# Attention and expert layers on one core: the value products of a head set in one visit instead of three

## The chip, the cores and the metric
One core of one Trainium2 chip runs the whole program. The metric is the device time of one execution in microseconds (us); the median of the runs is given. TensorE, VectorE, ScalarE, GpSimd and SyncE each run their own in-order stream and meet through semaphores.

## The reference, cut to what matters
Input x is 4 batches of 512 tokens with 128 channels, fp32. Attention has 16 heads of 8 channels, causal, with a slope per head added to the key position:

```
x = x + attention(layernorm(x)) ; x = x + ffn(layernorm(x))
scores = q k^T / sqrt(8) + slope[h] * key_position, masked above the diagonal
attn = softmax(scores);  y = attn v;  y @ w_proj + b_proj
ffn: top-1 gate of 8 experts is used only as a factor near 1;
     sum over all experts of gelu(z @ w1[e] + b1[e]) @ w2[e] + b2[e], times that factor
```

## The kernel before, in words
**Steps.** The kernel walks over batches b (4) and over sets s of four heads (4 sets, called SETS; the four heads of a set are its QUADS). One (b, s) is a step, n = 4b + s, so there are steps 0 to 15. Each step has 16 places; a plan written out by hand says at which place TensorE issues what. For set n the step does:

- twelve exponential units (`exp_unit`, lines 754 and 760): scores transposed (keys on partitions) into a bank of `a_ring` (three PSUM banks), a mask matmul in bf16 on top (line 760), and then ScalarE's exponential into `probs` (line 559). Four units (one for each head) make a kind. Kind 0 is key block 0 (512 query columns), kind 1 key blocks 1 and 3 (384 + 128), kind 2 key block 2 (256).
- the value products (`pv`, line 779): `probs` times `v_ones` (values and a column of ones for the denominator), 128 x 32 weights, four heads side by side in four column tiles of TensorE, into the one bank `pv_bank`. Two consecutive sets share the bank. fp32 matmuls are issued as two instructions each, so kind 0 is 8, kind 1 is 16 and kind 2 is 8 instructions.
- twelve maximum units for the set after it (`max_unit`, line 732): scores with queries on partitions into a bank of `v_ring` (three PSUM banks), and VectorE's maximum along the keys (line 1066, a custom instruction and a read-out of its accumulator for each query block). When all twelve are done, `transpose_max` (line 741, 16 columns of weights) turns the maxima, VectorE makes `m_hi` and `m_lo` (lines 1083, 1084), and SyncE's queue writes them into `q_stack` (line 389) for the next step's exponential units.
- parts of other batches (`side`): projection of the next batch's q, k, v (lines 685 to 687, with transposes on line 696), the transposes and the projection of y (lines 792, 799, 808), z (layer norm output, transposed on line 816, split by VectorE into `zT_hi` and `zT_lo` on lines 962 and 963), logits, and the FFN of the batch before: `ffn1` (three matmuls for each 128-column tile, lines 685 to 687, into `a_ring`, GELU on ScalarE, line 576) and `ffn2` (line 847, fp32). In steps 5 and later, `ffn1` tiles 0 and 1 of a step are at place 1, tiles 2 and 3 at place 2, tile 4 at place 4. Steps with b >= 1 and s = 2 have one tile; steps 13, 14, 15 have 2, 2 and 4. Tile 0 of a batch is in s = 1, and z is transposed at place 15 of s = 0 (steps 4, 8, 12).

Within a place the order on TensorE is: side work, maximum units, `transpose_max`, exponential units, `pv`. Steps 0 to 4 follow `EARLY_PLAN`, the others `LATER_PLAN`. In `LATER_PLAN` the last maximum unit is at place 11, the ninth exponential unit at 12, `transpose_max` at 13, the last exponential unit at 15.

**Value products now.** Kind 0 is issued at place 12 (11 in the early plan), kind 1 at place 15, and kind 2 (`pv_last`) at place 0 of the next step. A visit waits until the exponentials of its kind are done (`e_freed`). After the last kind `pv_done` is raised; ScalarE copies the bank after every second set (`evacuate_pv`, line 566), and the exponentials of set n wait for the `pv_done` of set n - 2, since `probs` has two buffers.

After step 15 come the remaining FFN tiles of batch 2, the y work of batch 3, and the whole FFN of batch 3.

Of the kernel before, what the change touches and what calls it, by code (L numbers as in the profile page):

```python
# [35 lines left out]
P = 128  # L36
QUADS = 4
QR = P // QUADS
# [8 lines left out]
KINDS = 3  # L47
# [15 lines left out]
PLACES = 16  # L63
EARLY_PLAN = {
    "max": (-1, 0, 2, 3, 4, 5, 6, 8, 8, 9, 11, 11), "take_max": (12,),
    "exp": (4, 4, 5, 6, 8, 8, 9, 11, 11, 13, 14, 14), "pv": (11, 15), "pv_last": (0,),
}
LATER_PLAN = {
    "max": (-1, -1, 2, 3, 4, 5, 6, 7, 8, 9, 10, 11), "take_max": (13,),
    "exp": (4, 5, 6, 7, 8, 9, 10, 10, 12, 13, 14, 15), "pv": (12, 15), "pv_last": (0,),  # L70
}

STAGES = {
# [25 lines left out]
def block_kernel(nc, x, w_attn, w_proj, w1, w2, columns, rows, consts, out):  # L99
    B, T, C = x.shape  # L100
# [4 lines left out]
    TB = T // P  # L105
    SETS = H // QUADS
    UNITS = KINDS * QUADS
# [8 lines left out]
    KEY_BLOCKS = [[0], [1, 3], [2]]  # L116
    KIND_AT = [0, 512, 1024]
    PCOLS = 1280

    with ExitStack() as ctx:  # L120
        def sb(name, shape, dt=F32):
            return ctx.enter_context(nc.sbuf_tensor(name, shape, dt))

        def bank(name):
            return ctx.enter_context(nc.psum_tensor(name, [P, 512], F32))

        def sem(name):
            return ctx.enter_context(nc.semaphore(name))
# [50 lines left out]
        v_ones = [sb(f"v_ones{i}", [P, TB, SETS, QUADS, QR]) for i in range(2)]  # L179
# [6 lines left out]
        probs = sb("probs", [P, 2, QUADS, PCOLS])  # L186
# [32 lines left out]
        pv_bank = bank("pv_bank")  # L219
# [29 lines left out]
        e_freed = sem("e_freed")  # L249
# [13 lines left out]
        pv_done = sem("pv_done")  # L263
# [27 lines left out]
        def next_set(b, s):  # L291

            return (b, s + 1) if s < SETS - 1 else (b + 1, 0)

        def plan(n):
            return EARLY_PLAN if n <= SETS else LATER_PLAN

        def planned(b, s, k, what):

            return [unit for unit, place in enumerate(plan(SETS * b + s)[what]) if place == k]  # L300

        def maxima_due(n, k):


            units = []
            for ahead in (1, 2):
                for unit, place in enumerate(plan(n + ahead - 1)["max"]):
                    at = place if (n + ahead) % SETS else max(place, 0)
                    if at == k - PLACES * (ahead - 1) and n + ahead < SETS * B:
                        units.append(((n + ahead) // SETS, (n + ahead) % SETS, unit))  # L310
            return units
# [350 lines left out]
        def _(pe):  # L662
# [55 lines left out]
            def max_unit(b, s, k):  # L718
                if k == 0 and b < 2 and s == 0:
                    pe.wait_ge(q_const, SETS * (b + 1))  # L720
                if k == 0 and b == 0 and s % 2 == 0:
                    pe.wait_ge(k_const, QUADS * (s // 2 + 1))
                if k == 0:
                    pe.wait_ge(q_loaded, q_count(b + 1))
                q, kind = k // KINDS, k % KINDS
                if kind == 0 and s % 2 == 0:
                    pe.wait_ge(k_loaded[s // 2][q], K_LOADS * (b + 1))
                    pe.wait_ge(k_low_loaded[s // 2][q], K_LOW_LOADS * (b + 1))
                dst = v_bank()
                at = 0  # L730
                for n in MAX_BLOCKS[kind]:
                    last = pe.matmul(dst[:, at:at + P * (n + 1)], q_stack[b % 2][:, s, n * P:(n + 1) * P],  # L732
                                     k_stack[:, s, q, 0:P * (n + 1)], start=True, stop=True)
                    at += P * (n + 1)
                last.then_inc(v_filled, 1)

            def transpose_max(b, s):
                n = SETS * b + s
                pe.wait_ge(max_ready, n + 1)
                dst = v_bank()  # L740
                pe.transpose(dst[0:TB * QUADS, 0:P], row_max[:, n % 2, :], ident).then_inc(v_filled, 1)  # L741
# [19 lines left out]
                          start=False, stop=True, skip_group_check=True).then_inc(e_filled, 1)  # L761


            def pv(b, s, kind):
                n = SETS * b + s
                pe.wait_ge(e_freed, UNITS * n + QUADS * (kind + 1))
                if kind == 0 and s == 0:
                    pe.wait_ge(v_ready, b + 1)
                    if b == 0:
                        pe.wait_ge(v_const, 2)  # L770
                    if b == 1:
                        pe.wait_ge(v_const, 4)
                if kind == 0 and s % 2 == 0 and n >= 2:
                    pe.wait_ge(pv_evacuated, n // 2)
                at = KIND_AT[kind]
                for j in KEY_BLOCKS[kind]:
                    cols = P * (TB - j)
                    for q in range(QUADS):
                        last = pe.matmul(pv_bank[QR * q:QR * (q + 1), j * P:T], v_ones[b % 2][:, j, s, q, :],  # L779
                                         probs[:, n % 2, q, at:at + cols],  # L780
                                         start=(s % 2 == 0 and j == 0), stop=(s % 2 == 1 and j == 2),
                                         tile_position=(0, QR * q), skip_group_check=True)
                    at += cols
                if kind == KINDS - 1:
                    last.then_inc(pv_done, 1)


            def transpose_y(b, half):
# [68 lines left out]
            def side(b, s, k):  # L857

                for stage, of in due(STAGES, b, s, k, B):
                    if stage == "y_low":  # L860
                        transpose_y(of, 0)
                    if stage == "y_high":
                        transpose_y(of, 1)
                    if stage == "y_norm":
                        transpose_y_norm(of)
                    if stage == "attention":
                        project_y(of)
                    if stage == "z":
                        transpose_z(of)
                    if stage == "logits":  # L870
                        logits(of)
                    if stage == "ffn":
                        transpose_ffn(of)
                    if stage == "x":
                        transpose_x(of)
                    if stage == "q":
                        project_qk(of, 0)
                    if stage == "k":
                        project_qk(of, 1)
                    if stage == "v":  # L880
                        project_v(of)
                fb, tiles = chunk(b, s)
                for m, at in zip(tiles, FFN1_AT):
                    if k == at:
                        ffn1(fb, m)
                for m, at in zip(tiles, FFN2_AT):
                    if k == at:
                        ffn2(fb, m)
# [12 lines left out]
            for b in range(B):  # L901
                for s in range(SETS):
                    n = SETS * b + s
                    for k in range(PLACES):
                        side(b, s, k)
                        for unit in maxima_due(SETS * b + s, k):
                            max_unit(*unit)
                        if planned(b, s, k, "take_max") and next_set(b, s)[0] < B:
                            transpose_max(*next_set(b, s))
                        for unit in planned(b, s, k, "exp"):  # L910
                            exp_unit(b, s, unit)
                        for kind in planned(b, s, k, "pv"):
                            pv(b, s, kind)
                        if planned(b, s, k, "pv_last") and n >= 1:
                            pv((n - 1) // SETS, (n - 1) % SETS, KINDS - 1)
            pv(B - 1, SETS - 1, KINDS - 1)

            tiles = range(sum(LAST_TILES), NT)
            for i, m in enumerate(tiles):
# [380 lines left out]
```

## Time and profile before

| | |
|---|---|
| median of 3 runs | 323.85 us (323.07 to 324.44) |
| the profiled execution's own time | 324.16 us |
| its span, first to last instruction | 322.4 us |
| TensorE (PE) busy in the span | 291.8 us, 91% |
| VectorE (DVE), ScalarE (ACT) busy | 190.1 us (59%), 193.9 us (60%) |
| `pv` matmuls (line 779) | x512, 42.3 us, mean 440 ns |
| granted TensorE clock, mean | 0.998 |

The span is 1.8 us shorter than the execution's time. Busy time of matmuls overlaps and has modelled ends, so the distance between the starts of two neighbouring rows is the better measure of what an instruction costs. Steps 0 to 15 run from about 36 us to 273 us of the span.

### The profile page before, as it was taken

What the parts mean: (1) busy time and instruction counts of PE and PEld (TensorE: products, weight loads), DVE (VectorE), ACT (ScalarE), POOL (GpSimd) and SP (SyncE); (2) the same over time, 40 slices, a digit from 0 to 9 for tenths busy, and PEclk for the clock granted to TensorE, in tenths of its full rate; (3) what the DMA queues carried; (4) which work ended last, traced back from release to release, by engine and by line L of the source; (5) the groups of instructions that cost most, each with busy time, mean ns of one, the idle gap of its engine ahead of it and who ended that gap; (6) DMA issues with size and microseconds to landing.
All of it is one profiled execution on the core that took longest, in us unless ns stands there. A gap on an engine that the chain in (4) does not pass through costs nothing.

```text
span 322.4 us, 5513 instructions
## 1 busy us (share of the span) xinstructions
PE 291.8 (91%) x1784; PEld 191.4 (59%) x1784; DVE 190.1 (59%) x788; ACT 193.9 (60%) x323; POOL 76.1 (24%) x211
## 2 busy tenths in 40 slices
PE   0638799999969999999999999999999999999993
PEld 0435465666646666667666676657667655655651
DVE  4528479778777768564777785647776711451011
ACT  6462245556447468758577397767587786525362
POOL 3349312520133055002321181020300500000120
PEclk9999999999999999999999999999999999999999
DMA  6254300130300013003000140011001000000001
GB/s 181 91 146 121 134 4 0 33 123 2 92 29 0 0 39 123 3 0 100 19 3 2 35 142 19 2 34 49 3 3 37 0 4 0 0 2 4 30 0 33
DMA packets 12524, 13.23 MB, mean 41 GB/s; under 512 B 2064, under 2 KB 9104, under 8 KB 12240
## 3 DMA queue, kind: packets, MB, share of 16 engines
q1 hardware_dynamic: 11376, 11.70, 12.0%
q0 software_dynamic: 1024, 1.05, 1.6%
q8 instruction: 14, 0.23, 0.3%
q10 hardware_dynamic: 96, 0.13, 0.2%
q14 instruction: 14, 0.11, 0.1%
HBM read 5.14 MB, written 1.05 MB: 19 GB/s over the span
## 4 chain that ended last, share of the span: by engine, by line
PE 81%; DVE 10%; DMA 3%; issue 2%; ACT 1%; SPq 1%; DVEq 0%; ACTq 0%
PE ffn_bank L847 17%; PE a_ring L754 12%; PE v_ring L732 12%; PE pv_bank L779 11%; PE a_ring L685 5%; PE a_ring L760 5%; PE a_ring L687 4%; PE a_ring L686 4%; DVE unused L1066 4%; PE v_ring L808 1%; DMA q_stack<-q_lo 1%; PE v_ring L685 1%; PE v_ring L741 1%; DMA q_stack<-m_lo 1%; PE v_ring L686 1%
## 5 line engine op out<-in xcount | busy, mean ns | idle before, releaser
L1066 DVE CUSTOM_DVE_ANT_0 unused<-v_ring,cst 128x512 bf16<-128x512 f32 (+3 forms) x256 | 112.1, 487 | 52.1 <-PE v_ring L732 48.0
L559 ACT ACTIVATE probs<-a_ring 128x512 f32<-128x512 f32 (+1 forms) x192 | 92.4, 526 | 67.6 <-PE a_ring L760 66.6
L732 PE MATMUL v_ring<-k_stack,q_stack 128*128 128x512 f32 (+3 forms) x256 | 88.5, 417 | 7.3 <-DMA q_stack<-q_lo 5.1
L754 PE MATMUL a_ring<-q_stack,k_stack 128*128 128x512 f32 (+3 forms) x256 | 76.6, 359 | 2.0 <-DMA q_stack<-m_lo 2.0
L847 PE MATMUL ffn_bank<-hidden,w_sb 128*128 128x512 f32 x128 | 66.3, 602 | 1.1 <-ACT ffn_T L585 0.8
L732 PEld LDWEIGHTS v_ring<-k_stack,q_stack 128*128 128x128 f32 x256 | 48.6, 206 | 27.5 <-issue 17.1
L576 ACT ACTIVATE hidden<-a_ring,cols_sb 128x512 f32<-128x512 f32 x64 | 43.4, 688 | 32.5 <-PE a_ring L687 32.0
L754 PEld LDWEIGHTS a_ring<-q_stack,k_stack 128*128 128x128 f32 x256 | 46.5, 196 | 9.5 <-issue 5.6
L760 PE MATMUL a_ring<-score_mask,ident_bf 128*128 128x128 bf16 (+1 forms) x192 | 47.9, 251 | 0.0
L779 PE MATMUL pv_bank<-probs,v_ones 128*32 128x256 f32 (+3 forms) x512 | 42.3, 440 | 0.0
L685 PE MATMUL a_ring<-zT_hi,w_hi 128*128 128x512 f32 x64 | 33.0, 516 | 0.8 <-DVEq L965 0.8
L326 POOL DMA_DIRECT2D k_stack<-k_lo x32 | 18.1, 568 | 56.3 <-PE a_ring L760 51.6
L760 PEld LDWEIGHTS a_ring<-score_mask,ident_bf 128*128 128x128 bf16 x192 | 18.7, 97 | 20.5 <-issue 13.1
L687 PE MATMUL a_ring<-zT_hi,w_lo 128*128 128x512 f32 x64 | 25.2, 393 | 0.0
L686 PE MATMUL a_ring<-zT_lo,w_hi 128*128 128x512 f32 x64 | 25.1, 393 | 0.0
L847 PEld LDWEIGHTS ffn_bank<-hidden,w_sb 128*128 128x128 f32 x128 | 21.5, 192 | 5.9 <-ACT hidden L576 3.1
L1066 DVE DVE_READ_ACCUMULATOR2_ANT row_max<- 128x1 f32 x256 | 21.3, 83 | 0.0
L685 PEld LDWEIGHTS a_ring<-zT_hi,w_hi 128*128 128x128 f32 x64 | 12.1, 188 | 11.3 <-issue 7.1
L779 PEld LDWEIGHTS pv_bank<-probs,v_ones 128*32 128x32 f32 x512 | 12.3, 109 | 9.8 <-issue 6.5
L332 POOL TENSOR_SCALAR var<-mean_square 128x4 f32<-128x4 f32 x4 | 0.8, 188 | 69.5 <-DVE mean_square L1132 69.4
L576 ACT ACT_TABLE_LOAD x13 | 16.7, 1283 | 0.2
L686 PEld LDWEIGHTS a_ring<-zT_lo,w_hi 128*128 128x128 f32 x64 | 12.1, 189 | 4.8 <-issue 3.6
(110 smaller groups left out, 289.5 us busy)
## 6 DMA issues: line engine op xcount, KB each, us to landing
q_stack<-q_hi SPq DMA_DIRECT2D x8, 256.0 KB
k_stack<-k_hi SPq DMA_DIRECT2D x60, 32.0 KB
x_in<-x SPq DMA_DIRECT2D x4, 256.0 KB, 4.0
hidden<-w SPq DMA_DIRECT2D x1, 1024.0 KB, 8.3
k_stack<-k_lo POOLq DMA_DIRECT2D x32, 32.0 KB, 2.3
q_stack<-q_lo SPq DMA_DIRECT2D x4, 256.0 KB
w_sb<-w SPq DMA_DIRECT2D x1, 1024.0 KB, 5.1
x_res<-x SPq DMA_DIRECT2D x4, 256.0 KB, 3.6
```

Source lines behind the costliest of these rows:

```text
L326: queue.dma_start(k_stack[ROW_Q * q + g::ROW_D, 2 * half:2 * half + 2, q, :].bitcast(F32), part[rows:rows + QR // 2, :].bitcast(F32)).then ...
L559: act.activation(probs[:, n % 2, q, KIND_AT[kind]:KIND_AT[kind] + cols], a_bank()[:, 0:cols], ACT.Exp).then_inc(e_freed, 1)
L576: act.activation(hidden[:, n % HB, :], a_bank()[:], ACT.Gelu, bias=b1_cols[:, m:m + 1]).then_inc(g_freed, 1)
L685: pe.matmul(dst, lhs[0], rhs[0], start=True, stop=False)
L686: pe.matmul(dst, lhs[0], rhs[1], start=False, stop=False)
L687: return pe.matmul(dst, lhs[1], rhs[0], start=False, stop=True)
L732: last = pe.matmul(dst[:, at:at + P * (n + 1)], q_stack[b % 2][:, s, n * P:(n + 1) * P], k_stack[:, s, q, 0:P * (n + 1)], start=True, stop ...
L754: pe.matmul(dst[:, at:at + P * (TB - j)], k_stack[:, s, q, j * P:(j + 1) * P], q_stack[b % 2][:, s, j * P:T], start=(at == 0), stop=False, ...
L760: pe.matmul(diagonal, ident_bf[:], score_mask[:].unsqueeze(1).to_broadcast([P, blocks, P]), start=False, stop=True, skip_group_check=True) ...
L779: last = pe.matmul(pv_bank[QR * q:QR * (q + 1), j * P:T], v_ones[b % 2][:, j, s, q, :], probs[:, n % 2, q, at:at + cols], start=(s % 2 == ...
L847: pe.matmul(ffn_bank[:], w2_sb[:, m, :], hidden[:, n % HB, :], start=(m == 0), stop=(m == NT - 1)).then_inc(ffn2_done, 1)
L1066: ins = dve.tensor_tensor_reduce(unused[:, (uses[0] - 1) % V_BANKS, at:at + cols], bank_[:, at:at + cols], cst[:, C_MASK + T - cols:C_MASK ...
```

## The change
`pv` loses its parameter `kind`: one call issues all 32 instructions of a set, and it waits for all twelve exponentials. The plans name one place, 1, and there the products of the set of the step before are issued, after the `ffn1` tiles of that place. The products of step 15 follow right after its last exponential unit. The number of matmuls, their shapes and their operands are the same; `pv_done` is raised once for each set as before.

```diff
 EARLY_PLAN = {
-    "exp": (4, 4, 5, 6, 8, 8, 9, 11, 11, 13, 14, 14), "pv": (11, 15), "pv_last": (0,),
+    "exp": (4, 4, 5, 6, 8, 8, 9, 11, 11, 13, 14, 14), "pv": (1,),
...
 LATER_PLAN = {
-    "exp": (4, 5, 6, 7, 8, 9, 10, 10, 12, 13, 14, 15), "pv": (12, 15), "pv_last": (0,),
+    "exp": (4, 5, 6, 7, 8, 9, 10, 10, 12, 13, 14, 15), "pv": (1,),
...
-            def pv(b, s, kind):
+            def pv(b, s):
                 n = SETS * b + s
-                pe.wait_ge(e_freed, UNITS * n + QUADS * (kind + 1))
-                if kind == 0 and s == 0:
+                pe.wait_ge(e_freed, UNITS * (n + 1))
+                if s == 0:
                     pe.wait_ge(v_ready, b + 1)
...
-                if kind == 0 and s % 2 == 0 and n >= 2:
+                if s % 2 == 0 and n >= 2:
                     pe.wait_ge(pv_evacuated, n // 2)
-                at = KIND_AT[kind]
-                for j in KEY_BLOCKS[kind]:
-                    cols = P * (TB - j)
-                    for q in range(QUADS):
-                        last = pe.matmul(...)
-                    at += cols
-                if kind == KINDS - 1:
-                    last.then_inc(pv_done, 1)
+                at = 0
+                for blocks in KEY_BLOCKS:
+                    for j in blocks:
+                        cols = P * (TB - j)
+                        for q in range(QUADS):
+                            last = pe.matmul(...)
+                        at += cols
+                last.then_inc(pv_done, 1)
...
-                        for kind in planned(b, s, k, "pv"):
-                            pv(b, s, kind)
-                        if planned(b, s, k, "pv_last") and n >= 1:
-                            pv((n - 1) // SETS, (n - 1) % SETS, KINDS - 1)
-            pv(B - 1, SETS - 1, KINDS - 1)
+                        if planned(b, s, k, "pv") and n >= 1:
+                            pv((n - 1) // SETS, (n - 1) % SETS)
+            pv(B - 1, SETS - 1)
```

## Rows read from the trace of the kernel before

**Rows 1.** Busy time by stretch (us, x instructions), clock, DMA share, GB/s.

```profile
142.00:211.00 69.00, 69.00 (x454) 46.12 (x446) 46.67 (x194) 47.41 (x79) 17.07 (x55) 1.00 0.13 38
```

The five pairs after the length of the stretch are TensorE's matmuls, its weight loads, VectorE, ScalarE and GpSimd.

**Rows 2.** Timeline of TensorE's matmuls, step 6: start, length, engine, line.

```profile
124.46 0.28 PE L760 MATMUL a_ring<-score_mask,ident_bf 128*128 128x256 bf16 x1
124.50 0.36 PE L732 MATMUL v_ring<-k_stack,q_stack 128*128 128x256 f32 x1
...
124.82 0.23 PE L760 MATMUL a_ring<-score_mask,ident_bf 128*128 128x128 bf16 x1
124.98 1.06 PE L779 MATMUL pv_bank<-probs,v_ones 128*32 128x512 f32 x8
125.98 0.28 PE L741 MATMUL v_ring<-cst,row_max 128*16 128x128 f32 x1
```

**Rows 3.** Timeline of VectorE in the same step.

```profile
125.25 0.08 DVE L1066 DVE_READ_ACCUMULATOR2_ANT row_max<- 128x1 f32 x1
```

**Rows 4.** Timeline around the kind-0 visits of steps 0 and 5.

```profile
43.18 1.07 PE L779 MATMUL pv_bank<-probs,v_ones 128*32 128x512 f32 x8
43.62 0.08 DVE L1066 DVE_READ_ACCUMULATOR2_ANT row_max<- 128x1 f32 x1
...
110.49 0.08 DVE L1066 DVE_READ_ACCUMULATOR2_ANT row_max<- 128x1 f32 x1
110.52 1.07 PE L779 MATMUL pv_bank<-probs,v_ones 128*32 128x512 f32 x8
```

**Rows 5.** Timeline in step 1, VectorE and TensorE (PEld is its weight load).

```profile
56.19 0.08 DVE L1066 DVE_READ_ACCUMULATOR2_ANT row_max<- 128x1 f32 x1
56.38 0.09 PEld L741 LDWEIGHTS v_ring<-cst,row_max 128*16 128x16 f32 x1 [0.39 <-DVEq L1075]
56.41 0.36 PE L754 MATMUL a_ring<-q_stack,k_stack 128*128 128x256 f32 x1
```

**Rows 6.** Timeline of TensorE at the boundary from step 6 to 7.

```profile
127.26 1.07 PE L779 MATMUL pv_bank<-probs,v_ones 128*32 128x384 f32 x16
128.26 0.74 PE L732 MATMUL v_ring<-k_stack,q_stack 128*128 128x512 f32 x3
128.94 0.64 PE L779 MATMUL pv_bank<-probs,v_ones 128*32 128x256 f32 x8
129.50 0.50 PE L685 MATMUL a_ring<-zT_hi,w_hi 128*128 128x512 f32 x1
```

**Rows 7.** Timeline of TensorE at the boundary from step 7 to 8.

```profile
144.96 1.50 PE L779 MATMUL pv_bank<-probs,v_ones 128*32 128x384 f32 x24
146.39 0.50 PE L685 MATMUL a_ring<-zT_hi,w_hi 128*128 128x512 f32 x1
...
147.19 0.39 PE L685 MATMUL a_ring<-zT_hi,w_hi 128*128 128x512 f32 x1
...
147.88 0.39 PE L685 MATMUL a_ring<-zT_hi,w_hi 128*128 128x512 f32 x1
```

**Rows 8.** Timeline around z, end of step 4 (first row) and step 8.

```profile
94.72 0.66 PE L816 MATMUL v_ring<-cst,z 128*128 128x128 f32 x4 [1.44 <-DVE z L979]
...
162.83 0.61 PE L816 MATMUL v_ring<-cst,z 128*128 128x128 f32 x4
...
163.92 0.23 PE L760 MATMUL a_ring<-score_mask,ident_bf 128*128 128x128 bf16 x1
...
164.20 0.69 DVE L963 TENSOR_TENSOR zT_lo<-v_ring,zT_hi 128x512 fp32r<-128x512 f32 x1
```

**Rows 9.** Timeline of the last batch's `zT` and the tile behind it.

```profile
288.00 0.69 DVE L963 TENSOR_TENSOR zT_lo<-v_ring,zT_hi 128x512 fp32r<-128x512 f32 x1
288.90 0.50 PE L685 MATMUL a_ring<-zT_hi,w_hi 128*128 128x512 f32 x1 [0.80 <-DVEq L965]
```

**Rows 10.** Timeline at the end of step 15, ScalarE and TensorE.

```profile
271.11 0.94 ACT L559 ACTIVATE probs<-a_ring 128x256 f32<-128x256 f32 x3 [1.00 <-PE a_ring L760]
...
271.33 0.23 PE L760 MATMUL a_ring<-score_mask,ident_bf 128*128 128x128 bf16 x1
```

More of the change, by code:

```diff
@@ L772, in pv @@
                         pe.wait_ge(v_const, 4)
-                if kind == 0 and s % 2 == 0 and n >= 2:
+                if s % 2 == 0 and n >= 2:
                     pe.wait_ge(pv_evacuated, n // 2)
-                at = KIND_AT[kind]
-                for j in KEY_BLOCKS[kind]:
-                    cols = P * (TB - j)
-                    for q in range(QUADS):
[L779 to L782, printed above, removed]
-                    at += cols
-                if kind == KINDS - 1:
-                    last.then_inc(pv_done, 1)
+                at = 0
[3 more added lines that the diff above has]
+                        for q in range(QUADS):
+                            last = pe.matmul(pv_bank[QR * q:QR * (q + 1), j * P:T], v_ones[b % 2][:, j, s, q, :],
+                                             probs[:, n % 2, q, at:at + cols],
+                                             start=(s % 2 == 0 and j == 0), stop=(s % 2 == 1 and j == 2),
+                                             tile_position=(0, QR * q), skip_group_check=True)
+                        at += cols
+                last.then_inc(pv_done, 1)
             def transpose_y(b, half):
```

## The prediction
> **What bounds the kernel now.** I read the busy time of each engine by stretch first, then TensorE's timeline around every visit of `pv` (the matmuls of line 779), then VectorE's and ScalarE's timelines beside it. In the stretch by stages TensorE is busy in all of it, at full clock, and VectorE and ScalarE for about two thirds [rows 1]. So inside the sixteen steps every microsecond that TensorE's in-order stream gains or loses is a microsecond of the kernel, and the timeline of TensorE can be added up from start to start of neighbouring rows. What the reader should look for is twofold: what a visit costs beyond its columns, and which results of other engines TensorE finds ready only because a visit stood ahead of the instruction that needs them.
>
> **What a visit costs.** A kind-0 visit takes 1.00 us from its first matmul to the next instruction (124.98 to 125.98) [rows 2]. Kinds 1 and 2 take 1.00 and 0.56 us apart (127.26 to 128.26, 128.94 to 129.50) [rows 6], and 1.43 us together (144.96 to 146.39) [rows 7]. Apart they cost 0.13 to 0.14 us more: that is the fixed part of a visit. One visit of all three kinds is then 1.00 + 1.43 - 0.14 = 2.29 us. Entering a visit after a mask matmul takes 0.16 us (124.82 to 124.98) where another matmul follows a mask after 0.04 us (124.46 to 124.50) [rows 2]: 0.12 us for the entry. After a visit the first FFN tile takes 0.80 us and the next one 0.69 us (146.39, 147.19, 147.88) [rows 7]: 0.11 us of exposed weight load. After a mask matmul most of that is paid anyway; I take 0.78 us there, bounds 0.69 and 0.80.
>
> Today there are 38 visits: 16 of kind 0, 10 of kinds 1 and 2 together (the same place 15 and place 0 with nothing between), and 6 steps where maximum units split them [rows 6]. Afterwards there are 16.
> The Trainium skill, "TensorEngine Tiling (Array Packing)", Key Properties, says that a change of tiling mode drains TensorE. Rows 2 agree in kind (0.12 us in, 0.14 us fixed), and by that rule alone 22 fewer visits would give 22 x 0.26 = 5.7 us, 318.4 us; it is a rival below. It overstates, because the visit that is left sits at a dearer place and L741 is a narrow-tile matmul too.
>
> **The stream of TensorE without waits.**
> Removed: kind 0 at place 11 or 12. In 14 steps L741 (`transpose_max`, 16 columns of weights) follows directly, and I assume that it pays the same entry after a mask as `pv` does, so exactly 1.00 us goes: 14.0 us. In steps 1 and 15 something else follows, so the entry goes too: 2 x 1.14 = 2.3 us. Sum 16.3 us.
> Added at the step boundaries. (a) Nine boundaries (into steps 5, 6, 8, 9, 10, 12 to 15), where kinds 1 and 2 stand together now. Before: entry 0.16, visit 1.43, tiles 0.80 + 0.69 + 0.69 = 3.77 us. After: 0.04, tiles 0.78 + 0.69, entry about 0.09 more than a tile's normal succession (the trace has no visit behind a tile; bounds 0 and 0.12), visit 2.29, next tile 0.80 = 4.69 us. So +0.92; where one or two tiles or a maximum unit follow, 0.86 to 0.90. Nine times 0.90 is 8.1 us. (b) Six boundaries (into steps 1 to 4, 7, 11), where the kinds are apart [rows 6]: 2.29 - 1.00 - 0.56 = +0.73, less one entry and an exposed load (0.12 to 0.20): +0.55 each, 3.3 us. (c) The end: kinds 1 and 2 become all three: +0.86. Sum 12.3 us.
> Net: -16.3 + 12.3 = -4.0 us. In a steady step it is only about -0.1 us, since the merged visit breaks a run of FFN tiles.
>
> **The waits that the moved matmuls cover now.**
> 1. `transpose_max` waits for VectorE's last maximum. In the step of rows 2 the last maximum matmul starts at 124.50, VectorE's last read-out runs from 125.25 to 125.33 [rows 3], and L741 comes at 125.98. Where L741 really waits, it starts 0.11 us after the read-out ends (56.19 + 0.08, then 56.38) [rows 5]. Without the kind-0 visit TensorE arrives at 124.98 and stands until 125.44: 0.46 us. The chain from maximum matmul over VectorE to L741 follows TensorE's own stream, so it doesn't shrink. Eight steps (6 to 8, 10 to 14) have this form: 3.7 us. In steps 5 and 9 the k projection stands in between: 110.57 + 0.11 - 110.52 = 0.16 us [rows 4], 0.3 us. In step 0 it is 43.70 + 0.11 - 43.18 = 0.63 [rows 4]; in steps 2 and 3 VectorE was behind by about 0.2 us more than its chain demands, and the later `pv` of the step before gives it back: 0.45 each, 0.9 us. Step 1: L741 waits for VectorE already, with a visit ahead of it [rows 5], so the 1.14 is lost, less the 0.15 or so of the later start: 1.0. Step 4: TensorE stands 1.44 us for z at its place 15 in any case [rows 8], so what it gains before that it waits there: 1.0. Sum 7.5 us.
> 2. FFN tile 0 of a batch waits for `zT`. It is at place 1 of step 1 of the batch, and z is transposed at place 15 just ahead. L816 starts at 162.83, the last mask at 163.92, so without a visit TensorE would arrive at the tile at 163.96; VectorE ends `zT_lo` at 164.20 + 0.69 = 164.89 [rows 8], and where a tile waited for it, it started 0.21 us later (288.69, 288.90) [rows 9]: 165.10. The 1.43 us visit covers that now. Afterwards the tile stands ahead of the visit and waits 1.14 us. Three steps (5, 9, 13): 3.4 us. L816 itself arrives 0.5 us earlier in two of them and may find z late, as it does in step 4 [rows 8]: I take 0.1 each, bounds 0 and 0.5.
> 3. `pv` waits for all twelve exponentials. Behind FFN tiles they are long done. At the end nothing stands between: the last three take 0.94 us on ScalarE, ending 0.72 us after the last mask started (271.33 to 272.05) [rows 10]; with the kind-0 visit gone they also queue behind the ninth, so I take 0.75 us beyond the entry (bounds 0.56 and 1.0). Boundaries into 1 to 4 have maximum units in front: 0.1 us each at most, 0.3 in all. Sum 1.0 us.
> Together 7.5 + 3.6 + 1.0 = 12.1 us.
> The Trainium skill, "TensorE: Matmul & The Clock Gate", The mechanism, states that matmuls start and end in strict program order, while weight loads may be pulled ahead. If matmuls could pass L741, item 1 would vanish. Rows 5 fit the rule: the next matmul comes 0.03 us behind the late L741, not before it.
>
> Nothing moves on the DMA queues: `pv` issues no DMA. SP's `load_max` follows VectorE's m values, which come up to 0.5 us earlier. ScalarE's copy of the finished bank waits for `pv_done` later, but its place is behind the tile exponentials or GELUs that precede it, and the first exponential of the step has the same distance from it as now: nothing, unless the table load slips (a rival). VectorE gets fewer results during the 2.29 us, and catches up.
>
> **Sum.** -4.0 + 12.1 = +8.1 us on the profiled execution's 324.16 us: 332.3 us. It stands 0.3 us above the median of the runs, 323.85; on that the forecast is 332.0 us.
>
> **The rivals.**
> A. The waits are absorbed (VectorE, less disturbed, delivers its maxima earlier, or the pauses only replace time in which TensorE waited for weights): the stream alone decides, -4.0 us, 319.9 us. For it: fewer visits, a measured fixed cost. Against it: the covered intervals of rows 3 and 8 are chains of dependent work behind TensorE itself. It decides once the waits are under 4.0 us in sum. By the rule of "TensorEngine Tiling (Array Packing)" in the Trainium skill the time would be 318.4 us in its place.
> B. Only part of the waits appears: L741's waits as computed, but the tile's wait for `zT` and the end's wait mostly hidden: -4.0 + 7.5 + about 1 = +4.5, 328.4 us. Against it: no other work stands between L816 and the tile.
> C. The 2.29 us block at place 1 starves ScalarE, and then FFN tiles or the first exponentials queue on the three `a_ring` banks behind ScalarE's table load: 0.3 us in each of eleven later steps, +3.4 more, 335.4 us. Against it: the GELUs of tiles 0 and 1 can run during the visit.
> D. The waits and the saving cancel: no change, 324 us. Nothing in the rows makes this sum likely.
>
> **How the numbers follow.** Forecast (330 to 334.5) 0.70, A 0.06, B 0.12, C 0.09, D 0.03. The unknown entries (eleven, 0 to 0.12) and the early steps are worth about 1.5 us either way. From 328.0 to 335.5 I leave out A, D and the outer parts of B and C. Within 0.5% means 322.2 to 325.5 us: faster 0.06, same 0.04, slower 0.90.
>
> **What would show it.** TensorE's busy share falls and waits for L741 on VectorE appear in nearly every step at about 0.4 to 0.5 us; `pv` shows 16 groups of 32 matmuls, each 2.29 us long; L685 waits for L965 three times at about 1.1 us; the matmul behind the last exponentials waits for ScalarE before the final visit. If L741 shows no waits, item 1 is wrong; if the visits are much shorter than 2.29 us, the fixed cost is larger than read here.

## The result, and the profile after

The changed kernel takes 335.41 us (median of 4 runs, 334.95 to 336.33), the kernel before beside it 324.14 us (4 runs, 323.07 to 324.62). The ratio is 1.0357, 95% interval [1.0337, 1.0377]: 3.6% slower. The profiled execution took 335.37 us with a span of 333.5 us, 11.2 us longer than before's. The forecast of 332.0 us had the direction and is 3.4 us short.

From the page of the changed kernel, busy time and the slices of the span:

```profile
span 333.5 us, 5513 instructions
PE 293.5 (88%) x1784; PEld 193.7 (58%) x1784; DVE 189.3 (57%) x788; ACT 194.3 (58%) x323; POOL 75.8 (23%) x211
PEclk9975599999958999999999999999999999999998
```

The instructions are the same in number, the share of TensorE fell from 91% to 88%. New is the "58" in the row of the granted clock: TensorE ran at its lower level in the middle of the steps.

The "755" ahead of it is the start of the program, up to 40.61 us, 4.6 us into step 0. Before's row has 9 there only because its record of the clock begins at 41.35 us. Its matmuls up to then are as slow: a 512-column matmul of L732 at 38.37 us takes 0.57 us to the next instruction, and 0.31 us at 41.46 us. So the mean clock of a run is low or high by whether the start is in its record (in all ten traces it goes by that): 0.962 to 0.966 or 0.998 to 0.999 in the kernel before, 0.950 or 0.980 to 0.981 in the changed one. Either way the changed kernel's is lower by 0.012 to 0.019, and 10.24 us at half clock in 333 us is 0.015. So a fall of that length fits the mean clock of all four runs of the changed kernel, though only one has a trace.

A stretch as long as that of [rows 1] (3 to 6 us further on in the steps than that one), the stretch just ahead of the fall, and the fall itself, by the view of stretches:

```profile
152.80:221.80 69.00, 66.63 (x421) 45.06 (x414) 46.24 (x190) 45.29 (x76) 15.27 (x52) 1.00 0.12 35
...
85.00:91.80 6.80, 4.87 (x34) 3.87 (x32) 6.14 (x28) 3.60 (x7) 1.83 (x10) 1.00 0.31 88
91.80:102.05 10.25, 8.47 (x32) 5.17 (x36) 5.58 (x22) 3.85 (x7) 3.31 (x18) 0.50 0.01 3
```

TensorE now has gaps in the steady steps, 66.63 of 69.00 us where it had none. From 91.81 to 102.05 us it is granted 0.50, which is the 1.2 GHz level in place of 2.4 GHz. The same window of the kernel before:

```profile
91.80:102.05 10.25, 8.81 (x66) 5.91 (x59) 6.86 (x28) 5.99 (x12) 3.65 (x19) 1.00 0.01 3
```

66 matmul instructions then, 32 now, in the same 10.25 us.

The view of waits on TensorE: what was waited for, us in all, times, the longest.

```profile
PE v_ring L741 <- DVEq L1074: 6.9, 14, 0.9
PE a_ring L685 <- DVEq L964: 3.7, 4, 1.0
...
PE v_ring L817 <- DVE z L978: 0.9, 1, 0.9
...
PE pv_bank L781 <- ACT probs L559: 0.5, 1, 0.5
```

These are the three items of waiting that the prediction lists. First, 6.9 us at `transpose_max`. One wait of these lies ahead of step 0 and was there before, as the timelines of the kernel before and of the changed one show:

```profile
30.61 0.38 PE L741 MATMUL v_ring<-cst,row_max 128*16 128x128 f32 x1 [0.95 <-DVEq L1075]
...
30.66 0.38 PE L741 MATMUL v_ring<-cst,row_max 128*16 128x128 f32 x1 [0.95 <-DVEq L1074]
```

So 6.0 us are new. Second, 3.7 us at the tile behind `zT`, of which 0.8 us is the last batch's, there before too [rows 9], so 2.9 us are new. Third, 0.5 us at the last visit. The view counts idle time from the modelled end of the matmul ahead, so a wait is a little longer from start to start.

The timeline of step 6, TensorE and one row of VectorE, for [rows 2] and [rows 3]:

```profile
129.63 0.23 PE L760 MATMUL a_ring<-score_mask,ident_bf 128*128 128x128 bf16 x1
...
130.06 0.08 DVE L1065 DVE_READ_ACCUMULATOR2_ANT row_max<- 128x1 f32 x1
...
130.26 0.28 PE L741 MATMUL v_ring<-cst,row_max 128*16 128x128 f32 x1 [0.39 <-DVEq L1074]
130.29 0.36 PE L754 MATMUL a_ring<-q_stack,k_stack 128*128 128x256 f32 x1
```

From the mask to L741 it takes 0.63 us (129.63 to 130.26) where the mask, its visit and L741 took 1.16 us (124.82 to 125.98). So 0.53 us is gained for the 1.00 us visit that left; the prediction had 1.00 - 0.46 = 0.54. L741 comes 0.12 us after VectorE's read-out has ended (130.14), as the forecast had it (0.11). From start to start the wait is 0.47 us (0.63 less the 0.16 of an entry), which the view has as 0.39.

TensorE at the boundary from step 7 to 8, for [rows 7]:

```profile
149.16 0.23 PE L760 MATMUL a_ring<-score_mask,ident_bf 128*128 128x128 bf16 x1
...
150.44 0.39 PE L687 MATMUL a_ring<-zT_hi,w_lo 128*128 128x512 f32 x1
150.75 2.36 PE L781 MATMUL pv_bank<-probs,v_ones 128*32 128x512 f32 x32
153.04 0.50 PE L685 MATMUL a_ring<-zT_hi,w_hi 128*128 128x512 f32 x1
153.84 0.40 PE L685 MATMUL a_ring<-zT_hi,w_hi 128*128 128x512 f32 x1
```

The visit takes 2.29 us (150.75 to 153.04), as added up from its parts. The tile behind it takes 0.80 us (to 153.84). The first visit matmul comes 0.31 us after L687 (150.44 to 150.75).

The timeline around z in step 8, for [rows 8]:

```profile
168.82 0.23 PE L760 MATMUL a_ring<-score_mask,ident_bf 128*128 128x128 bf16 x1
169.18 0.69 DVE L962 TENSOR_TENSOR zT_lo<-v_ring,zT_hi 128x512 fp32r<-128x512 f32 x1
170.08 0.50 PE L685 MATMUL a_ring<-zT_hi,w_hi 128*128 128x512 f32 x1 [1.02 <-DVEq L964]
```

The tile starts 1.26 us after the mask (168.82 to 170.08); a matmul after a mask takes 0.04 us, so it stands 1.2 us. The forecast was 1.14 us.

The timeline at the end of step 15, for [rows 10]:

```profile
280.40 1.31 ACT L559 ACTIVATE probs<-a_ring 128x256 f32<-128x256 f32 x4 [0.20 <-PE a_ring L760]
...
281.07 0.23 PE L760 MATMUL a_ring<-score_mask,ident_bf 128*128 128x128 bf16 x1
281.77 2.36 PE L781 MATMUL pv_bank<-probs,v_ones 128*32 128x512 f32 x32 [0.47 <-ACT probs L559]
284.06 0.50 PE L685 MATMUL a_ring<-zT_hi,w_hi 128*128 128x512 f32 x1
```

The visit starts 0.70 us after the mask where a visit without a wait starts 0.16 us after it: 0.54 us, for which 0.75 was taken (low bound 0.56).

**Where the 11.2 us arise.** The table gives, for one mask matmul in each step, its start after less its start before: the mask of the first exponential unit of the step. The change is that since the row above. The forecast column has the prediction's own terms for the same stretch, added up.

| up to the start of | measured shift | change | forecast |
|---|---|---|---|
| step 0 | -0.09 | | |
| step 4 | -0.27 | -0.2 | +0.9 |
| step 5 | +4.72 | +5.0 | +2.0 |
| step 8 | +5.29 | +0.6 | +0.4 |
| step 9 | +7.08 | +1.8 | +1.6 |
| step 12 | +8.18 | +1.1 | +0.4 |
| step 13 | +9.92 | +1.7 | +1.6 |
| step 15 | +10.68 | +0.8 | +0.7 |
| the last instruction | +11.16 | +0.5 | +0.5 |

One row stands out: from the start of step 4 to that of step 5, 5.0 us where 2.0 were expected. That is where the clock fell. TensorE there, by its timeline:

```profile
89.84 0.73 PE L732 MATMUL v_ring<-k_stack,q_stack 128*128 128x384 f32 x3 [1.25 <-DVE row_max L1065]
...
91.89 0.38 PE L741 MATMUL v_ring<-cst,row_max 128*16 128x128 f32 x1 [0.77 <-DVEq L1074]
...
94.40 1.12 PE L817 MATMUL v_ring<-cst,z 128*128 128x128 f32 x4 [0.87 <-DVE z L978]
...
97.18 0.80 PE L685 MATMUL a_ring<-zT_hi,w_hi 128*128 128x512 f32 x1 [0.81 <-DVEq L964]
...
100.04 3.33 PE L781 MATMUL pv_bank<-probs,v_ones 128*32 128x512 f32 x32
103.30 0.50 PE L685 MATMUL a_ring<-zT_hi,w_hi 128*128 128x512 f32 x1
```

TensorE waits for VectorE 1.25 us, then 0.77 us at `transpose_max`, and that wait is new. The clock falls as it ends. The waits for z and for `zT` follow at the lower level. The visit, which begins at the lower level and ends at the upper one, takes 3.26 us (100.04 to 103.30) in place of 2.29 us.

### The profile page after: what moved, and what is told of

It is laid out like the page before. It is cut to its first block, busy times and chain, and to the rows that moved or that the text cites. A ratio compares the mean times of both kernels' runs of the same rounds, so it can differ in the third digit from the quotient of the medians.

```text
span 333.5 us, 5513 instructions
## 1 busy us (share of the span) xinstructions
PE 293.5 (88%) x1784; PEld 193.7 (58%) x1784; DVE 189.3 (57%) x788; ACT 194.3 (58%) x323; POOL 75.8 (23%) x211
## 3 DMA queue, kind: packets, MB, share of 16 engines
q1 hardware_dynamic: 11376, 11.70, 11.2%
## 4 chain that ended last, share of the span: by engine, by line
PE 66%; DVE 19%; issue 4%; POOL 3%; DMA 3%; ACT 2%; SPq 1%; DVEq 0%; POOLq 0%; ACTq 0%
PE ffn_bank L848 13%; PE pv_bank L781 11%; DVE unused L1065 8%; PE v_ring L732 8%; PE a_ring L754 8%; PE a_ring L685 5%; PE a_ring L687 4%; PE a_ring L686 4%; PE a_ring L760 3%; DVE stats L969 1%; DMA q_stack<-q_lo 1%; PE v_ring L809 1%; PE v_ring L741 1%; DMA q_stack<-m_lo 1%; PE v_ring L685 1%
## 5 line engine op out<-in xcount | busy, mean ns | idle before, releaser
L732 PE MATMUL v_ring<-k_stack,q_stack 128*128 128x512 f32 (+3 forms) x256 | 87.9, 419 | 7.5 <-DMA q_stack<-q_lo 5.6
L732 PEld LDWEIGHTS v_ring<-k_stack,q_stack 128*128 128x128 f32 x256 | 48.8, 208 | 27.3 <-issue 18.5
L781 PE MATMUL pv_bank<-probs,v_ones 128*32 128x256 f32 (+3 forms) x512 | 38.7, 444 | 0.5 <-ACT probs L559 0.5
L685 PE MATMUL a_ring<-zT_hi,w_hi 128*128 128x512 f32 x64 | 34.1, 533 | 3.7 <-DVEq L964 3.7
L781 PEld LDWEIGHTS pv_bank<-probs,v_ones 128*32 128x32 f32 x512 | 14.5, 111 | 22.2 <-issue 20.1
L687 PE MATMUL a_ring<-zT_hi,w_lo 128*128 128x512 f32 x64 | 25.7, 401 | 0.0
```

What stands on the lines that cost most here:

```text
L685: pe.matmul(dst, lhs[0], rhs[0], start=True, stop=False)
L687: return pe.matmul(dst, lhs[1], rhs[0], start=False, stop=True)
```

## The experiments

In the kernels below one function says at which place the products of set m run; 16 and more is in the next step. All kinds at 17 is the changed kernel, and two experiments keep that and edit something else.

```
VISITS_EARLY = ((0,), 11), ((1,), 15), ((2,), 16)      # as before, sets 0 to 4
VISITS_LATER = ((0,), 12), ((1,), 15), ((2,), 16)      # as before, sets 5 to 15
ONE_VISIT = ((0, 1, 2), 17),
def visits(m):
    return ONE_VISIT
```

Times are medians with the ratio to the kernel before on the same chip and its 95% interval.

| kernel | us (runs) | ratio | clock fall in steps 4 and 5, profiled execution |
|---|---|---|---|
| changed | 335.41 (4) | 1.0357 [1.0337, 1.0377] | 91.81 to 102.05 |
| kind 0 stays | 329.88 (4) | 1.0155 [1.0104, 1.0207] | none |
| step 4 old | 330.45 (4) | 1.0190 [1.0164, 1.0216] | none |
| step 4 alone new | 328.64 (4) | 1.0141 [1.0113, 1.0169] | 92.90 to 103.14 |
| maxima issued at place 14 | 336.01 (4) | 1.0369 [1.0346, 1.0392] | 92.53 to 102.77 |
| kind 0 stays, step 4 old | 326.37 (6) | 1.0059 [1.0040, 1.0077] | none |
| filler in step 4 | 333.61 (4) | 1.0292 [1.0272, 1.0313] | none |
| visit ahead of tile 0 | 330.78 (4) | 1.0216 [1.0190, 1.0242] | 94.06 to 97.47 |
| pairs joined | 323.03 (9) | 0.9958 [0.9943, 0.9973] | none |

**Kind 0 stays.**

```diff
-    return ONE_VISIT
+    return ((0,), 11 if m <= 4 else 12), ((1, 2), 17)
```

> The changed kernel, but kind 0 stays where it was (place 11 or 12); kinds 1 and 2 go in one visit at place 1. Theory (each visit costs its fixed part, and the kind-0 visit covers TensorE's wait for the last maximum): no waits of L741, so against the kernel before: six boundaries 0.3 us cheaper, nine 0.05 dearer, three waits for zT of 1.1 us, 0.5 at the end, no fall of the clock near 92 us: +2.5 us, ratio about 1.008. Rival (moving the products to place 1 is what costs, by the gap it tears into the FFN tiles or by starving ScalarE): still at least +8 us, ratio 1.025.

329.88 us, with runs far apart: 326.68 for the profiled execution, and 329.69, 330.07 and 330.24. Its waits on TensorE:

```profile
PE a_ring L695 <- DVEq L982: 3.9, 4, 1.2
...
PE v_ring L751 <- DVEq L1092: 1.0, 1, 1.0
```

L751 is `transpose_max` here. With kind 0 in its old place it waits once, at 30.81 us ahead of step 0, as before; the waits for `zT` stay. So the kind-0 visit was what covered the maxima, and item 1 is shown. The trace ends 2.5 us after that of before, which is the forecast's number, but by luck in part: its clock rose at 39.41 us, and 1.1 us of lead stands in it by the sixth exponential unit of step 0, ahead of any moved product. The change costs 3.6 us there. The profiled execution has no fall of the clock in the steps. The three others take 3.0 to 3.6 us more, and their mean clocks are 0.957, 0.955 and 0.955 where it has 0.965. That is 6 to 7 us more at the lower level, so they hold no fall of 10.24 us on top of the same start. Whether it lies in step 4 or at the start is open: in the kernel before, which has no fall in its trace, a mean clock of 0.962 in place of 0.965 or 0.966 goes with 1 us more. The median of 329.88 us and the forecast of +2.5 us therefore can't be set against each other.

**Step 4 old, the rest new**, and **step 4 new, the rest old.**

```diff
-    return ONE_VISIT
+    return VISITS_EARLY if m == 4 else ONE_VISIT
```

> The changed kernel, but the set of step 4 keeps its three visits (places 11, 15 and 0). Theory (the clock falls to half at 92 us because step 4 has no visit between its waits any more): the fall of 10.24 us is gone, and with it 3 us; the wait for zT of step 5 and the larger visit there go too: 5 us under the changed kernel, about 330.4 us, ratio to the kernel before 1.020. Rival (the fall has another cause, or comes at any such time): the clock still falls once for 10 us, only 2 us less, about 333.4 us, ratio 1.029.

```diff
-    return ONE_VISIT
+    return ONE_VISIT if m == 4 else VISITS_EARLY if m < 4 else VISITS_LATER
```

> The kernel before, with only the set of step 4 in the new form (one visit, at place 1 of step 5). Theory (the same): the clock falls to half near 92 us, and this one step costs +5 us of the +11.2: about 329 us, ratio 1.015. Rival (the fall needs the shorter waits of the steps ahead as well, or is chance): no fall, +2 us, ratio 1.006.

Step 4 alone decides 4 to 5 us: undoing one set of sixteen takes 335.41 to 330.45 us, and changing one set of sixteen brings 324.26 to 328.64 us. The two parts add up: +6.2 us (ratio 1.0190) and +4.4 us make 10.6 us of the 11.3. With step 4 old the stretch of the fall has 66 matmuls at a granted clock of 1.00, as in the kernel before. With step 4 alone new the fall begins at 92.90, and the view of stretches shows:

```profile
91.80:102.05 10.25, 7.59 (x28) 4.55 (x32) 5.88 (x24) 4.01 (x8) 3.36 (x17) 0.55 0.01 3
```

Every other step of that kernel is the old one, and its trace loses 5.4 us between the starts of step 4 and step 5. The mean clocks of the runs agree with the two traces: 0.965, 0.966 and twice 0.999 with step 4 old, as in the kernel before, and 0.980 and three times 0.953 with step 4 alone new.

**The maxima taken later.** `transpose_max` goes from place 12 or 13 to 14, behind more exponential units, which were to cover its wait.

```diff
 EARLY_PLAN = {
...
-    "take_max": (12,)
+    "take_max": (14,)
...
 LATER_PLAN = {
...
-    "take_max": (13,)
+    "take_max": (14,)
```

> The changed kernel, with transpose_max at place 14 in both plans (it was at 12 and 13), so that the ninth and, in the later plan, an FFN product stand between the last maximum and L741. Theory (L741's waits are time on the path): the ten waits of steps 5 to 14 go (about 4 us), the early ones shrink by 0.2 each: 4.5 us under the changed kernel, about 331 us, ratio to the kernel before 1.022, with the fall of the clock still there. Rival (the wait only moves: to the m values' way into q_stack, or to the next maximum units): no gain, 335 us, ratio 1.035.

336.01 us: no gain. The theory missed, and the rival came. The waits at L751 (`transpose_max`) did shrink, from 6.2 to 1.2 us (counting the two short ones that the view leaves out, and without the 0.95 us ahead of step 0), and others came in their place, 4.8 us in all:

```profile
PE v_ring L751 <- DVEq L1092: 2.1, 4, 1.0
PE v_ring L834 <- DVE z L996: 2.5, 3, 1.5
PE v_ring L742 <- issue: 1.2, 1, 1.2
PE v_ring L742 <- DVEq L1176: 0.7, 1, 0.7
```

L742 is the maximum unit and L834 the transpose of z. What comes after `transpose_max` on VectorE comes later too: z, the side work, and, as it looks, with it the maxima of the next set, for whose `v_ring` banks TensorE waits. Most of the new waits are again on VectorE. The 1.2 us at L742, in step 3, the view can't put down to any engine, and 0.5 us are on ScalarE.

**Kind 0 stays and step 4 is old.**

```diff
-    return ONE_VISIT
+    if m == 4:
+        return VISITS_EARLY
+    return ((0,), 11 if m <= 4 else 12), ((1, 2), 17)
```

> Kind 0 stays at its place and kinds 1 and 2 go in one visit at place 1 as in e1_kind0_stays, but the set of step 4 keeps its three visits. In e1 the profiled execution had no fall of the clock in the steps and took 326.68 us, the three others had one more and took about 330. Theory (the fall hangs on TensorE's pauses in steps 4 and 5, which e1 lengthens by the wait for zT): with step 4 as it was no execution has it, and the time is that of e1's profiled execution less step 4's share of 1.5 us: about 325.3 us, ratio 1.003, all runs within 1 us. Rival (the fall comes by chance or in any step with a wait for zT): again two groups of times 3.5 us apart.

326.37 us, its six runs within 1.7 us (325.45 to 327.12): 1.1 us more than forecast, and a wider spread than the 1 us. The split of the first experiment into 326.7 and about 330 us is gone, and that fits a fall of the clock in steps 4 and 5 that came in some of its runs. The spread that is left goes with the start: 325.45 and 325.53 us at a mean clock of 0.967, 326.82 and 327.12 at 0.959 (the latter is the trace, which has a longer start and no fall). What is left is 2.1 us, and the view of waits has the rest of items 2 and 3 for it:

```profile
PE a_ring L697 <- DVEq L984: 2.7, 3, 1.0
...
PE pv_bank L793 <- ACT probs L571: 0.5, 1, 0.5
```

Of the 2.7 us 0.8 are the last batch's, so 1.9 us are the `zT` waits of steps 9 and 13, and 0.5 us is the end.

**A filler in step 4.** The changed kernel with four needless 512-column matmuls into the bank of `transpose_max`, ahead of its wait, in one step. `transpose_max` then overwrites the bank; nothing is left out. The edit also puts the wait for the bank ahead of the wait for the maxima, and that in every step.

```diff
-                pe.wait_ge(max_ready, n + 1)
                 dst = v_bank()
+                if n == 5:
+                    pe.wait_ge(w1_split, 2)
+                    for _ in range(4):
+                        pe.matmul(dst[:], w1_hi[:, 0:P], w1_hi[:, 0:T], start=True, stop=True)
+                pe.wait_ge(max_ready, n + 1)
```

> The changed kernel with four needless matmuls of 512 columns ahead of step 4's transpose_max, while it waits for VectorE (they write its own PSUM bank, which the transpose then overwrites; nothing else is changed). Theory (the fall of the clock needs TensorE idle in that pause): it is gone, -3 us, about 332.4 us, though work was added. Rival (the fall comes from the order of the value products, or the pause alone doesn't decide it): the clock still falls for 10.24 us, 335.4 us or more.

333.61 us, 1.8 us less than the changed kernel, with more work. TensorE in step 4:

```profile
90.62 1.18 PE L753 MATMUL v_ring<-w_hi 128*128 128x512 f32 x4
91.63 0.27 PE L755 MATMUL v_ring<-cst,row_max 128*16 128x128 f32 x1
...
94.09 0.66 PE L838 MATMUL v_ring<-cst,z 128*128 128x128 f32 x4 [1.51 <-DVE z L1000]
...
96.42 0.50 PE L695 MATMUL a_ring<-zT_hi,w_hi 128*128 128x512 f32 x1 [1.20 <-DVEq L986]
```

The fillers (L753) take 1.0 us where TensorE stood, L755 (`transpose_max`) starts within 0.04 us of where it does in the changed kernel (91.63 and 91.89, and this trace is 0.30 us ahead by then), and the clock stays at its upper level. The mean clocks of the four runs (0.967 and 0.999, each twice) have no fall either. The waits for z and `zT` are 1.51 and 1.20 us, against 0.87 and 0.81 us at the lower clock: the fall hid 1.0 us of its own price in waits that were there anyway. The first exponential's mask of step 5 comes 3.00 us earlier than in the changed kernel, that of step 4 0.30 us earlier: the fall costs 2.7 us. Of the 3.00 us 0.7 are lost again by the end (2.3 us), and that is the other half of the edit: with the two waits in the new order `transpose_max` comes 0.09 us later behind its mask in each other step (0.72 and not 0.63 us in step 6). So the 1.8 us between the medians is the price of the fall less that. Work in the wait ahead of 91.8 us is enough to keep the clock up, with the visit that follows left where it is. That the wait alone is enough to bring the clock down doesn't follow; see the next experiment.

The Trainium skill, "TensorE: Matmul & The Clock Gate", What's actually happening, says that half rate is the default and that recent activity of TensorE releases it. The traces agree: needless activity kept the clock up, with 2.7 us for it in this kernel.

**The visit ahead of tile 0.** In the three steps whose tile 0 waits for `zT`, the visit goes to place 0.

```diff
-    return ONE_VISIT
+    return (((0, 1, 2), 16),) if m in (4, 8, 12) else ONE_VISIT
```

> The changed kernel, but the products of steps 4, 8 and 12 are issued at place 0 of the step behind, ahead of the FFN tiles, the others at place 1. Theory (these tiles wait 1.1 us for zT, which a visit ahead of them covers, at the price of about 0.5 us of waiting for the last exponentials): 0.9 us less for each of the three, 332.6 us, with the fall of the clock still there, since it begins before that visit. Rival 1 (the visit takes away the fall too): about 329.6 us. Rival 2 (the wait for the exponentials eats it): 335 us.

330.78 us, 4.6 us less than the changed kernel. In the timeline of the boundary into step 9:

```profile
165.91 0.23 PE L770 MATMUL a_ring<-score_mask,ident_bf 128*128 128x128 bf16 x1
166.61 2.36 PE L791 MATMUL pv_bank<-probs,v_ones 128*32 128x512 f32 x32 [0.47 <-ACT probs L569]
168.90 0.50 PE L695 MATMUL a_ring<-zT_hi,w_hi 128*128 128x512 f32 x1
```

The tile's wait is gone, and the visit waits for the last exponentials in its place: 0.7 us less at steps 9 and 13 each, not 1.2. At step 5 it is 2.5 us less; that holds the same cover and a fall of the clock that lasts 3.41 us and not 10.24. Why it begins later and ends sooner the runs don't settle.

Theory and rival 1 both came, in different runs of one program. The run with a mean clock of 0.986, which is 9 us at the lower level, took 332.66 us, the theory's time. The two with 1.000 took 330.55 and 330.58 us, 1.0 us more than rival 1's 329.6: they have no fall at all. Up to the end of step 4 this kernel issues what the changed kernel issues, and TensorE stands as long there (1.27 us for the maxima, 0.77 us at `transpose_max`, 1.56 us for z). So these waits don't bring the fall in every run. The wait for `zT`, which the visit covers here, has a part in whether it comes, or chance has. Of the 4.6 us only 1.4 are from the cover at steps 9 and 13; the rest is the cover at step 5 and the fall that is shorter or missing.

**The pairs joined.** The forecast's fixed part alone: kinds 1 and 2 are joined at place 0 in the six boundaries where maximum units split them, and kind 0 and all else stay as before; 32 visits in place of 38.

```diff
-    return ONE_VISIT
+    early = m <= 4
+    if m in (0, 1, 2, 3, 6, 10):
+        return ((0,), 11 if early else 12), ((1, 2), 16)
+    return VISITS_EARLY if early else VISITS_LATER
```

> The kernel before, where only kind 1 of steps 0 to 3, 6 and 10 moves from place 15 to place 0, next to kind 2, so that 38 visits become 32 and nothing that covered a wait is moved. Theory (a visit costs its fixed part, entry and the exposed weight load, 0.25 to 0.45 us here): six visits less give -2 us, ratio 0.994. Rival (what a visit costs is hidden, or the exponentials are late for the joined visit): no change, ratio 1.000.

323.03 us (9 runs, 321.99 to 323.53) against 324.29 us (16 runs): 1.3 us and 0.4% [0.3, 0.6] faster than the kernel before, where 2 us were expected. The traces are 2.2 us apart, but 1.0 us of that is there by the sixth exponential unit of step 0, ahead of any moved instruction (this clock rose at 39.44 us, before's at 41.35). The other 1.2 us are at the boundaries: into steps 7 and 11 0.23 us each (the shift goes from -1.72 to -1.95 and from -1.95 to -2.18 us), into step 3 0.52, into step 4 0.24, into steps 1 and 2 nothing. So a visit less gave about its fixed cost or more at four of six boundaries where no cover was lost, and nothing at two. Why not there the runs don't show.

## Why the prediction was right and where it fell short

**The stream of TensorE** stands. All sixteen visits are of 32 matmuls, and all but the one at the lower clock take 2.29 us. That L741 pays the same entry after a mask as `pv` isn't shown: wherever it follows a mask it waits, and the wait hides the entry. The assumed entry behind a tile, 0.09 us more than the normal succession, is 0.08: 0.31 us from L687 to the visit, 0.23 us from L687 to what follows it elsewhere (185.39 to 185.62 in step 9).

**Item 1**, 7.5 us expected: 6.0 us of new idle time in the view, and in a steady step, from start to start, the size forecast (0.47 for 0.46). Kind 0 back in place removes it.

**Item 2**, 3.6 us: 2.9 us in three waits. Up to the starts of steps 9 and 13, 1.8 and 1.7 us are lost for the 1.6 forecast. In step 5, at the lower clock, the wait is 0.81 us; in the filler's kernel, at the upper one, it is 1.20.

**Item 3**, 1.0 us: 0.5 us, at the end alone. In the early steps the visit doesn't wait.

**The step that failed is the first conclusion of the argument: from "busy in all of it, at full clock" [rows 1] to "So inside the sixteen steps every microsecond that TensorE's in-order stream gains or loses is a microsecond of the kernel".** From it followed a sum with no term for the clock. The waits were priced by their own length only, and what they do to the matmuls after them was left out. Rows 1 are from 142 to 211 us. In step 4 TensorE had already been standing, 1.44 us for z [rows 8], and for VectorE's maxima ahead of that; there the new wait of 0.77 us at `transpose_max` brought the clock down for 10.24 us: work in that wait keeps it up. The filler prices the fall at 2.7 us; step 4 put back takes it away (together with 2 us of waits), and step 4 alone brings it. With 2.7 us for it the forecast would have been 334.7 us.

Two smaller errors went opposite ways.

Early steps, 0.9 us expected by the start of step 4, -0.2 measured: 1.1 us too dear. About 0.3 of it is from the start and not from the change (the clock reached its upper level at 40.61 us, at 41.35 in before, and step 0 has gained 0.3 us by its sixth exponential unit, ahead of the place where kind 0 was). The waits at L741 in steps 2 and 3 were some 0.2 us longer each than taken. What was really missed is at the boundaries into steps 1 to 3: 0.3, 0.1 and 0.2 us, for 0.6 each. Before, at the boundary into step 3, behind the kind-2 visit:

```profile
71.95 0.30 PEld L732 LDWEIGHTS v_ring<-k_stack,q_stack 128*128 128x128 f32 x2 [0.41 <-DVE row_max L1066]
71.95 1.24 PE L732 MATMUL v_ring<-k_stack,q_stack 128*128 128x256 f32 x4
72.70 0.30 PEld L732 LDWEIGHTS v_ring<-k_stack,q_stack 128*128 128x128 f32 x2 [0.44 <-DVE row_max L1066]
73.03 0.45 PE L754 MATMUL a_ring<-q_stack,k_stack 128*128 128x512 f32 x1
```

and after the change:

```profile
69.51 2.36 PE L781 MATMUL pv_bank<-probs,v_ones 128*32 128x512 f32 x32
71.80 0.86 PE L732 MATMUL v_ring<-k_stack,q_stack 128*128 128x256 f32 x4
...
72.50 0.45 PE L754 MATMUL a_ring<-q_stack,k_stack 128*128 128x512 f32 x1
```

Four maximum matmuls took 1.08 us to the next unit (71.95 to 73.03) because the weight loads of the second pair (72.70) waited for VectorE to free `v_ring`; after the change the four go in one piece. Within a group of matmuls that wait is counted as busy. While the 2.29 us visit runs VectorE catches up, and they take 0.70 us. The prediction's sentence "VectorE gets fewer results during the 2.29 us, and catches up" was right and had no price.

Steps 5 to 15 were taken 1.2 us too cheap, 6.4 measured for 5.25. The z steps (8 and 12) make 0.3 of it. Step 9 makes 0.45: behind `transpose_max` the first k projection comes 0.67 us after L855 and not 0.37, which looks like another wait for a bank inside the busy time. The rest is 0.05 to 0.1 us in each step.

In sum: 8.1 - 1.1 (early steps) + 2.7 (the clock) + 0.25 (the rest of step 4) + 1.2 (later steps) = 11.1 us; the trace has 11.2.

**The rivals.** A and D are out: the waits were not absorbed. B is out, since the tile's and the end's waits came. C gave 335.4 us, and that is what was measured, but not by its mechanism: it wanted 0.3 us more in each of eleven later steps and waits on ScalarE. The waits view has 0.5 us for the exponentials in all, and the missing time is in step 4. So it is luck that the wide range, whose upper end of 335.5 us stood for part of C, still holds 335.41 us; the range of the forecast itself, 330 to 334.5 us, doesn't.

**What stays open.** In the kernel with kind 0 kept, it isn't known where the other three runs were at the lower clock. In the changed kernel the place of the fall is known from one trace; the mean clocks of the three others fit one as long. With the visit ahead of tile 0 the fall comes in some runs, at another moment and shorter, and in two not at all. So the wait at `transpose_max` in step 4 is needed for it, by the filler (a fall in none of four runs, for all four without it), but what else decides is not known.

## What to carry to other kernels

A short piece of work just ahead of an instruction that needs another engine's result may be worth its own length in cover: here 22 visits less save 4 us of TensorE's stream by the sum, and uncover 6.0 + 2.9 + 0.5 us of waits by the view. Taking the maxima later only moved them. Read every stage of the profile and not a steady one alone: where TensorE already stands for a microsecond, one more short wait can cost its clock for ten. Set traces against each other only from a point behind their starts: here two of them had a lead of 1.0 and 1.1 us from the start alone. And join pieces where nothing is covered by their being apart; that was worth 1.3 us here.

## What the runs showed of the hardware

- After waits of 1.25 and 0.77 us in step 4 TensorE was granted 0.50 of its clock for 10.24 us (91.81 to 102.05), though it was busy for 4.87 of the 6.80 us ahead. The stretch is equally 10.24 us in two other kernels, and 3.41 us in a third. Of that third one's four runs two have a mean granted clock of 1.000, and so no fall.
- Ten microseconds at half clock cost 2.7 us. TensorE stood for 1.7 us of them (0.87 and 0.81), the waits were 1.0 us shorter than at the upper clock, and a row of an FFN tile came 0.43 us after the one before (98.09 to 98.52, with step 4 alone new) where it takes 0.23 at the upper level.
- Four needless matmuls of 1.0 us in all, in a wait, made the changed kernel 1.8 us faster, although the same edit made `transpose_max` 0.09 us later in each other step.
- That 0.09 us is the order of two waits: with the wait for the bank ahead of the one for the maxima, `transpose_max` comes 0.72 us after its mask in step 6, with the other order 0.63 us.
- Before 41.35 us the trace of the kernel before has no record of the clock, and its page prints full clock there; the matmuls take 0.57 us where they later take 0.31.
